# Low halves of the context keys in the recurrence stage: made by GpSimd in place of VectorE

## The chip, the cores and the metric

The kernel runs on one core of a Trainium2 chip. The metric is the device time of one execution in microseconds (us). Five engines work side by side on the core: TensorE (PE in the profile), VectorE (DVE), ScalarE (ACT), GpSimd (POOL) and SyncE (SP), which here issues the DMAs. Each runs its own instructions in order and waits on semaphores for what other engines made.

## The reference, cut to what matters

The program is four layers in a row. Layer 0 is a recurrent layer over 4 sequences of 512 positions; layers 1, 2 and 3 attend to a context of 1601 positions of width 512 for each sequence (layer 3 to the context and its own 512 latents together). The stage that is changed computes the recurrence of layer 0 and, beside it, the keys and values that the three attention layers need of the context.

```python
# layer 0: state s (head, 16, 16), one step per position
def step(s, rkvw):
    r_t, k_t, v_t, w_t = rkvw
    a = k_t[:, :, :, None] * v_t[:, :, None, :]
    out = jnp.einsum('bhk,bhkd->bhd', r_t, u * a + s)
    return (a + w_t[:, :, :, None] * s, out)
...
# layer 1: keys and values of the normalised context
a = _layer_norm(audio_kv, ln_gamma, ln_beta)
K = (a @ Wk.T); V = (a @ Wv.T)
# layer 2: of the context itself, eight key heads of 16
k = encoder_hidden_state @ Wk + bk
v = encoder_hidden_state @ Wv + bv
# layer 3: of the context itself
kv = h @ kv_w + kv_b
```

## The kernel before, in words

The program is a chain of stages, each a block of its own with a barrier behind it. The changed one is `scan_and_keys` (L1087). Two streams of work share its engines.

The first is the recurrence, in 256 steps (`STEPS`, 16 for each of 16 pieces of sequence and channel chunk; the pieces are numbered q). Step n handles 128 channels by 512 positions of one state column. TensorE spreads a value row over the partitions (`scan_vb`, L1282). VectorE multiplies it by the key (`outer`, `scan_a`, L1581, one operand in PSUM) and runs the scan over the 512 positions (`scan`, `scan_states`, L1588, operands in SBUF). GpSimd multiplies the state by the receptance (`weigh_state`, `scan_z`, L1511, operands in SBUF), and TensorE sums four of those products at a time (`reduce_four`, `scan_acc`, L1299). ScalarE seeds the first column of each state buffer two steps ahead (`seed`, L1376). There are `SR` = 4 state buffers, so the scan of step n waits for the product of step n-4, the seed of step n+2 for the product of step n-2, and the sum of products 4g to 4g+3 stands in TensorE's order at step 4g+5.

The second stream makes keys and values of the context. The 1601 positions of a sequence are cut into three tiles of 512 and one of 65, so there are 16 tiles, twelve full ones and four short. For each tile TensorE runs groups of float16 matmuls into one of three PSUM banks: `k2`, four `v2`, `std`, four `k3`, the `mean` of the next tile, four `v3`, four `k1`, four `v1` (`group_order`, L1057). The matmuls take float32 numbers as two float16 halves, a high one (the number rounded) and a low one (what is left). ScalarE drains each bank twice for a key: once in float32 (`scan_kf`, `scan_k2f`, L1384) and once rounded to float16 (`scan_hi`, `scan_k2hi`, L1385). `key_low` then subtracts the two and writes the low half in float16 (`scan_lo`, `scan_k2lo`, L1644). It is called once per key and tile: for k3 and k1 over 4 x n numbers a partition, for k2 over n. SyncE stores both halves (`keys_out`, L1203), and ScalarE may overwrite `kf` once the low half is made (semaphore `halves`).

Other work of the second stream on VectorE is the low half of the raw tile (`scan_xl`, L1625), centring (`scan_xc`, L1620), the reciprocal of the deviation (`scan_std`, L1630), the scaling by it (`scan_xc`, L1632) and the low half of the normalised tile (`a_low`, `scan_al`, L1637). On GpSimd it is the sum of channel chunks for mean and deviation: `add_pairs` (`scan_pairsum`, L1517) and `add_halves` (`scan_total`, L1524).

The order is written out by hand. `when[t, group, m]` gives every group a step by its share of TensorE's work, and each engine has a generator `keys` that yields the step at which its next piece is due. An engine first issues its part of the recurrence for step n and then whatever is due, so a piece stands behind the product or the scan of its step in the engine's order. The yields of one generator come in a fixed sequence: a piece whose step is earlier than the one before it in the generator still comes behind it. The places that matter are `yield when[t.t, "k3", C - 1] + 2`, `yield when[t.t, "k1", C - 1] + 2` and `yield when[t.t, "k2", 0] + 2`.

Of the kernel before, what the change touches and what calls it, by code (L numbers as in the profile page):

```python
# [7 lines left out]
ALU, ACT, AX = mybir.AluOpType, mybir.ActivationFunctionType, mybir.AxisListType  # L8
# [3 lines left out]
C = E // P  # L12
# [1074 lines left out]
def scan_and_keys(nc, w, k):  # L1087


    with ExitStack() as ctx:  # L1090
# [4 lines left out]
        tiles = [Stretch(t) for t in range(B * TILES)]  # L1095
        LAST = len(tiles) - 1

        ends, when, cost, count = {}, {}, {}, 0
# [12 lines left out]
        def end(t, what, m=None):  # L1111
            return ends[t, what, {"k": C - 1, "v": len(tiles[t].width) - 1}[what[0]] if m is None and what != "k2" else m or 0]
# [19 lines left out]
        xc, kf = ph.sb("xc", [P, C, KT]), ph.sb("kf", [P, C, KT])  # L1132
        hi, lo = ([ph.sb(f"{n}{i}", [P, C, KT], F16) for i in range(2)] for n in ("hi", "lo"))
        k2f, k2hi, k2lo = ph.sb("k2f", [P, 1, KT]), ph.sb("k2hi", [P, 1, KT], F16), ph.sb("k2lo", [P, 1, KT], F16)
# [19 lines left out]
        product, drained, copied = ph.sem("product"), ph.sem("drained"), ph.sem("copied")  # L1154
        staged, whigh, wlow = [ph.sem(f"staged{i}") for i in range(6)], ph.sem("whigh"), ph.sem("wlow")
        arrived = [ph.sem(f"arrived{i}") for i in range(2)]
        centred, squared, inverted, normed, scaled = (ph.sem(n) for n in ("centred", "squared", "inverted", "normed", "scaled"))
        paired, totalled = ph.sem("paired"), ph.sem("totalled")
        xhigh, xsplit, asplit, halves = ph.sem("xhigh"), ph.sem("xsplit"), ph.sem("asplit"), ph.sem("halves")
        kstored = {n: ph.sem(f"stored_{n}") for n in ("k1", "k2", "k3")}  # L1160
# [13 lines left out]
        with nc.Block() as block:  # L1174
# [329 lines left out]
            @block.gpsimd  # L1504
            def _(pool):
                def weigh_state(n):
                    pool.wait_ge(scanned, n + 1)
                    pool.wait_ge(seeded, n + 1)
                    if n >= ZR:
                        pool.wait_ge(reduced, (n - ZR) // 4 + 1)  # L1510
                    nc.gpsimd.tensor_tensor(Z[n % ZR][:], src["r"][n // HS % 2][:], S[n % SR][:, 0:T], ALU.mult).then_inc(zdone, 1)  # L1511

                def add_pairs(t, nth):
                    n, done = t.n, 2 * t.t + nth
                    if done:
                        pool.wait_ge(totalled, done)
                    nc.gpsimd.tensor_tensor(pairsum[:, :, 0:n], x[t.t % 2][:, 0:2, 0:n], x[t.t % 2][:, 2:4, 0:n], ALU.add).then_inc(paired, 1)  # L1517

                def add_halves(t, nth):
                    n, done = t.n, 2 * t.t + nth  # L1520
                    pool.wait_ge(paired, done + 1)
                    if t.t:
                        pool.wait_ge(product, end(t.t - 1, ("mean", "std")[nth], 0))
                    nc.gpsimd.tensor_tensor(total[nth][:, 0:n], pairsum[:, 0, 0:n], pairsum[:, 1, 0:n], ALU.add).then_inc(totalled, 1)  # L1524

                def keys():
                    yield 6
                    pool.wait_ge(arrived[0], 16)
                    add_pairs(tiles[0], 0)
                    add_halves(tiles[0], 0)  # L1530
                    yield 11
                    pool.wait_ge(squared, 1)
                    add_pairs(tiles[0], 1)
                    add_halves(tiles[0], 1)
                    for t in tiles[1:]:
                        before = tiles[t.t - 1]
                        yield when[before.t, "k3", 0]
                        pool.wait_ge(arrived[t.t % 2], 16 * (t.t // 2 + 1))
                        add_pairs(t, 0)
                        yield when[before.t, "k3", 0] + 1  # L1540
                        add_halves(t, 0)
                        yield when[before.t, "k1", 2] + 3
                        pool.wait_ge(squared, t.t + 1)
                        add_pairs(t, 1)
                        yield when[before.t, "k1", 2] + 4
                        add_halves(t, 1)

                more = keys()
                due = next(more)
                for n in range(STEPS + AFTER):  # L1550
                    if n < STEPS:
                        weigh_state(n)
                    while due is not None and due <= n:
                        due = next(more, None)

            @block.vector
            def _(dve):
# [50 lines left out]
                def weight_low(j):  # L1608
                    name, stage = stages[j]
                    dve.wait_ge(whigh, j + 1)  # L1610
                    nc.vector.scalar_tensor_tensor(W[name].lo[:], stage, WSCALE, W[name].hi[:], ALU.mult, ALU.subtract).then_inc(wlow, 1)
# [24 lines left out]
                    dve.wait_ge(scaled, 2 * C * (t.t + 1))  # L1636
                    nc.vector.tensor_tensor(as_.lo[:, :, 0:n], xc[:, :, 0:n], as_.hi[:, :, 0:n], ALU.subtract).then_inc(asplit, 1)  # L1637

                def key_low(t, name, full, hi_, lo_):
                    n = t.n  # L1640
                    dve.wait_ge(drained, end(t.t, name))
                    if t.t:
                        dve.wait_ge(kstored[name], 32 * t.t)
                    nc.vector.tensor_tensor(lo_[:, :, 0:n], full[:, :, 0:n], hi_[:, :, 0:n], ALU.subtract).then_inc(halves, 1)  # L1644

                def keys():
                    for j in range(4):
                        yield STAGE_AT[j]
                        weight_low(j)
                    yield 9  # L1650
                    centre(tiles[0])
                    yield 10
                    x_low(tiles[0])
                    yield STAGE_AT[4]
                    weight_low(4)
                    yield STAGE_AT[5]
                    weight_low(5)
                    for t in tiles:
                        yield when[t.t, "k2", 0] + 2
                        key_low(t, "k2", k2f, k2hi, k2lo)  # L1660
                        yield when[t.t, "std", 0] + 2
                        normalise(t)
                        yield when[t.t, "k3", C - 1] + 2
                        key_low(t, "k3", kf, hi[0], lo[0])
                        yield when[t.t, "v3", min(1, len(t.width) - 1)] + 2
                        a_low(t)
                        if t.t < LAST:
                            yield when[t.t, "k1", 0]
                            x_low(tiles[t.t + 1])
                            yield when[t.t, "k1", 0] + 1  # L1670
                            centre(tiles[t.t + 1])
                        yield when[t.t, "k1", C - 1] + 2
                        key_low(t, "k1", kf, hi[1], lo[1])

                outer(0)
                more = keys()
                due = next(more)
                for n in range(STEPS + AFTER):
# [2457 lines left out]
```

## Time and profile before

| what | value |
|---|---|
| time, median of 3 runs | 5353.01 us (5352.04 to 5363.05) |
| the profiled execution | 5354.71 us |
| its span, first to last instruction | 5352.7 us |
| first scan of the stage starts, last one starts | 431.1 us, 1341.5 us |
| busy over the whole span: PE, DVE, ACT, POOL | 4758.5, 3731.0, 2930.4, 2071.8 us |
| granted TensorE clock, mean over the span | 0.946 |

The stage takes about 915 us of the 5352.7. A busy time is the time in which the engine had an instruction begun and not ended. For VectorE and GpSimd an instruction can be begun and stand still, so its recorded length is more than its work; the rows below show this. The idle time before an instruction is put down to the engine that released it.

### The profile page before, as it was taken

To read this page: it belongs to the slowest core of one execution; us is meant where nothing else is said; L and a number is where in the kernel's file an instruction comes from. 1 tells how busy PE (TensorE), PEld (TensorE's weight loads), DVE (VectorE), ACT (ScalarE), POOL (GpSimd) and SP (SyncE) were. 2 spreads that over 40 slices of the span, in tenths; PEclk is the share of its full clock that TensorE was granted. 3 is DMA by queue.
4 is the path that set the end of the run, shared out by engine and by line. 5 is a ranking of instruction groups with operands and counts; after the bars stand their busy time and mean duration, and the time that the engine had idled before them with its cause. 6 is when DMAs were issued, how large, how long until landed. Compare 5 with 4: busy or idle time off the path is not lost. (4 is left out here: it accounts for less than half of the span.)

```text
span 5352.7 us, 75036 instructions
## 1 busy us (share of the span) xinstructions
PE 4758.5 (89%) x28626; PEld 1687.4 (32%) x28626; DVE 3731.0 (70%) x4661; ACT 2930.4 (55%) x5439; POOL 2071.8 (39%) x924
## 2 busy tenths in 40 slices
PE   5995988999378799997899999997899999996899
PEld 2342433334133233332322222222343333331344
DVE  5658999999565677771599999993457777771431
ACT  2443444444344366664288888885226666665442
POOL 0005666666131388775000000000007888886000
PEclk9997999999699799998999999998999999998999
DMA  2334344343301433323211111112424233221200
GB/s 98 132 117 128 114 109 112 104 114 98 114 32 48 89 69 69 71 58 104 75 29 33 34 34 32 34 30 70 112 75 102 60 68 71 60 49 68 71 24 16
DMA packets 474607, 391.60 MB, mean 73 GB/s; under 512 B 174895, under 2 KB 372372, under 8 KB 474216
## 3 DMA queue, kind: packets, MB, share of 16 engines
q1 hardware_dynamic: 474240, 386.74, 26.7%
q8 instruction: 227, 3.72, 0.3%
q14 instruction: 140, 1.15, 0.1%
HBM read 246.24 MB, written 139.34 MB: 72 GB/s over the span
## 5 line engine op out<-in xcount | busy, mean ns | idle before, releaser
L2941 DVE TENSOR_REDUCE att_part<-att_scores 128x2 f32<-128x802 f32 x1024 | 953.6, 987 | 112.0 <-PE att_scores L2780 100.2
L2914 ACT ACTIVATE att_prob<-att_lower 128x512 f32<-128x512 f32 (+1 forms) x1664 | 883.7, 596 | 132.2 <-PE att_lower L2794 110.9
L3711 DVE TENSOR_REDUCE att_part<-att_scores 128x1 f32<-128x423 f32 x1280 | 676.0, 590 | 240.9 <-PE att_scores L3442 240.7
L3655 ACT ACTIVATE att_prob<-att_lower 128x512 f32<-128x512 f32 (+1 forms) x1088 | 563.2, 602 | 243.9 <-PE att_lower L3454 242.1
L3695 POOL TENSOR_TENSOR att_acc<-att_acc,att_prob 128x1024 f32<-128x1024 f32 (+2 forms) x240 | 671.3, 2797 | 51.6 <-ACT att_prob L3655 22.4
L2517 DVE TENSOR_REDUCE att_part<-att_scores 128x1 f32<-128x401 f32 x1024 | 515.3, 567 | 162.0 <-PE att_scores L2331 161.9
L1511 POOL TENSOR_TENSOR scan_z<-scan_r,scan_states 128x512 f32<-128x512 f32 x256 | 469.7, 1839 | 360.0 <-DVE scan_states L1588 347.9
L2809 PE MATMUL att_lower<-att_prob,att_v 128*32 128x256 f32 (+1 forms) x6144 | 526.0, 415 | 19.7 <-issue 19.7
L2456 ACT ACTIVATE att_prob<-att_scores 128x512 f32<-128x512 f32 (+1 forms) x832 | 430.7, 601 | 195.3 <-PE att_scores L2343 195.3
L2928 POOL TENSOR_TENSOR att_out<-att_sums_sb,att_spread 128x512 f32<-128x512 f32 x32 | 40.7, 1272 | 1170.5 <-DMA att_spread<-recips 1170.5
L2497 POOL TENSOR_TENSOR att_acc<-att_acc,att_prob 128x1024 f32<-128x1024 f32 (+2 forms) x176 | 450.3, 2559 | 68.6 <-ACT att_prob L2456 56.2
L2780 PE MATMUL att_scores<-att_k,att_q 48*128 48x401 f16 x2048 | 426.0, 341 | 29.1 <-DVE att_part L2941 25.5
L3442 PE MATMUL att_scores<-att_k,att_q 97*128 97x423 f16 x1280 | 434.9, 347 | 12.0 <-DVE att_part L3711 11.6
L2794 PE MATMUL att_lower<-att_q,att_k 49*128 49x512 f16 (+1 forms) x1664 | 421.5, 389 | 8.6 <-ACT att_prob L2914 1.5
L1588 DVE TENSOR_TENSOR_SCAN scan_states<-scan_w,scan_initial,scan_a 128x512 f32<-128x512 f32 x256 | 425.1, 1661 | 0.0
L3454 PE MATMUL att_lower<-att_q,att_k 98*128 98x512 f16 (+1 forms) x1088 | 409.6, 383 | 13.5 <-ACT att_prob L3655 7.6
L2331 PE MATMUL att_scores<-att_k,att_q 97*128 97x401 f16 x1024 | 357.6, 353 | 28.6 <-DMA att_q<-in_c_q 28.3
L2343 PE MATMUL att_scores<-att_q,att_k 98*128 98x512 f16 (+1 forms) x832 | 312.0, 382 | 6.3 <-ACT att_prob L2456 6.1
L3465 PE MATMUL att_lower<-att_prob,att_v 128*32 128x512 f32 (+1 forms) x2176 | 289.6, 604 | 0.0
L2354 PE MATMUL att_sums<-att_prob,att_v 128*32 128x512 f32 (+1 forms) x1664 | 221.4, 604 | 0.0
L3695 POOL TENSOR_TENSOR att_acc<-att_prob 128x2048 f32<-128x2048 f32 x16 | 72.6, 4537 | 374.4 <-ACT att_prob L3655 374.4
L3442 PEld LDWEIGHTS att_scores<-att_k,att_q 97*128 97x128 f16 x1280 | 124.7, 97 | 279.6 <-DVE att_part L3711 174.2
(397 smaller groups left out, 7875.8 us busy)
## 6 DMA issues: line engine op xcount, KB each, us to landing
v<-scan_val SPq DMA_DIRECT2D x96, 256.0 KB, 2.3
att_v<-v SPq DMA_DIRECT2D x32, 768.0 KB
att_spread<-recips SPq DMA_DIRECT2D x64, 256.0 KB
mix_plane<-in_mask SPq DMA_DIRECT2D x16, 800.5 KB, 6.5
att_k<-k1hi SPq DMA_DIRECT2D x32, 400.2 KB
att_k<-k3hi SPq DMA_DIRECT2D x32, 400.2 KB
scan_x<-in_ctx_t SPq DMA_DIRECT2D x12, 1024.0 KB, 6.0
o<-att_out SPq DMA_DIRECT2D x32, 256.0 KB, 2.0
```

The source lines that it names most:

```text
L1511: nc.gpsimd.tensor_tensor(Z[n % ZR][:], src["r"][n // HS % 2][:], S[n % SR][:, 0:T], ALU.mult).then_inc(zdone, 1)
L2456: nc.scalar.activation(prob[g % NP][0:kw(kt), h, :], scores2[0:kw(kt), n % RING2, :], ACT.Exp).then_inc(exped, 1)
L2497: nc.gpsimd.tensor_tensor(acc[s % 2][0:kw(kt), heads], so_far[0:kw(kt), heads], prob[g % NP][0:kw(kt), heads], ALU.add).then_inc(padded, 1)
L2517: nc.vector.reduce_max(part[q % 2][:, hc, piece:piece + 1], scores1[:, bank["piece", p], 0:PIECE], AX.X).then_inc(reduced, 1)
L2780: ins = nc.tensor.matmul(scores1[:, b, a, 0:PIECE], Q[i][r, e, c * P:(c + 1) * P], K[i][r, k0:k0 + PIECE], start=True, stop=True)
L2809: ins = nc.tensor.matmul(sums[32 * h:32 * h + 32, cols], V[s % 2][0:kw(kt), kt, :], prob[g % NP][0:kw(kt), h, cols], start=kt == 0, stop=k ...
L2914: nc.scalar.activation(prob[g % NP][0:kw(kt), h, :], scores2[0:kw(kt), n % RING2, :], ACT.Exp).then_inc(exped, 1)
L2941: nc.vector.reduce_max(part[q % 2][:, :, ec, piece], scores1[:, bank["unit", p], :, 0:PIECE], AX.X).then_inc(reduced, 1)
L3442: nc.tensor.matmul(scores1[:, b, 0:PIECE], Q[i][0:TOP, h, c * P:(c + 1) * P], K[i][0:TOP, h, k0:k0 + PIECE], start=True, stop=True).then_i ...
L3655: nc.scalar.activation(prob[g % NP][0:kw(kt), h, :], scores2[0:kw(kt), n % RING2, :], ACT.Exp).then_inc(exped, 1)
L3695: nc.gpsimd.tensor_tensor(acc[s % 2][0:kw(kt), heads], so_far[0:kw(kt), heads], prob[g % NP][0:kw(kt), heads], ALU.add).then_inc(padded, 1)
L3711: nc.vector.reduce_max(part[q % 2][:, hc, piece:piece + 1], scores1[:, bank["piece", p], 0:PIECE], AX.X).then_inc(reduced, 1)
```

## The change

`key_low` moves from VectorE's block to GpSimd's, with the same operands and the same semaphores, and so do its three calls for each tile. GpSimd's generator now runs over all tiles with the key halves at the steps that they had on VectorE. VectorE's generator loses them.

```diff
--- before.py
+++ after.py
@@ -1516,6 +1516,13 @@
                         pool.wait_ge(totalled, done)
                     nc.gpsimd.tensor_tensor(pairsum[:, :, 0:n], x[t.t % 2][:, 0:2, 0:n], x[t.t % 2][:, 2:4, 0:n], ALU.add).then_inc(paired, 1)
 
+                def key_low(t, name, full, hi_, lo_):
+                    n = t.n
+                    pool.wait_ge(drained, end(t.t, name))
+                    if t.t:
+                        pool.wait_ge(kstored[name], 32 * t.t)
+                    nc.gpsimd.tensor_tensor(lo_[:, :, 0:n], full[:, :, 0:n], hi_[:, :, 0:n], ALU.subtract).then_inc(halves, 1)
+
                 def add_halves(t, nth):
                     n, done = t.n, 2 * t.t + nth
                     pool.wait_ge(paired, done + 1)
@@ -1532,18 +1539,26 @@
                     pool.wait_ge(squared, 1)
                     add_pairs(tiles[0], 1)
                     add_halves(tiles[0], 1)
-                    for t in tiles[1:]:
-                        before = tiles[t.t - 1]
-                        yield when[before.t, "k3", 0]
-                        pool.wait_ge(arrived[t.t % 2], 16 * (t.t // 2 + 1))
-                        add_pairs(t, 0)
-                        yield when[before.t, "k3", 0] + 1
-                        add_halves(t, 0)
-                        yield when[before.t, "k1", 2] + 3
-                        pool.wait_ge(squared, t.t + 1)
-                        add_pairs(t, 1)
-                        yield when[before.t, "k1", 2] + 4
-                        add_halves(t, 1)
+                    for before in tiles:
+                        t = tiles[before.t + 1] if before.t < LAST else None
+                        yield when[before.t, "k2", 0] + 2
+                        key_low(before, "k2", k2f, k2hi, k2lo)
+                        if t:
+                            yield when[before.t, "k3", 0]
+                            pool.wait_ge(arrived[t.t % 2], 16 * (t.t // 2 + 1))
+                            add_pairs(t, 0)
+                            yield when[before.t, "k3", 0] + 1
+                            add_halves(t, 0)
+                        yield when[before.t, "k3", C - 1] + 2
+                        key_low(before, "k3", kf, hi[0], lo[0])
+                        if t:
+                            yield when[before.t, "k1", 2] + 3
+                            pool.wait_ge(squared, t.t + 1)
+                            add_pairs(t, 1)
+                            yield when[before.t, "k1", 2] + 4
+                            add_halves(t, 1)
+                        yield when[before.t, "k1", C - 1] + 2
+                        key_low(before, "k1", kf, hi[1], lo[1])
 
                 more = keys()
                 due = next(more)
@@ -1636,13 +1651,6 @@
                     dve.wait_ge(scaled, 2 * C * (t.t + 1))
                     nc.vector.tensor_tensor(as_.lo[:, :, 0:n], xc[:, :, 0:n], as_.hi[:, :, 0:n], ALU.subtract).then_inc(asplit, 1)
 
-                def key_low(t, name, full, hi_, lo_):
-                    n = t.n
-                    dve.wait_ge(drained, end(t.t, name))
-                    if t.t:
-                        dve.wait_ge(kstored[name], 32 * t.t)
-                    nc.vector.tensor_tensor(lo_[:, :, 0:n], full[:, :, 0:n], hi_[:, :, 0:n], ALU.subtract).then_inc(halves, 1)
-
                 def keys():
                     for j in range(4):
                         yield STAGE_AT[j]
@@ -1656,12 +1664,8 @@
                     yield STAGE_AT[5]
                     weight_low(5)
                     for t in tiles:
-                        yield when[t.t, "k2", 0] + 2
-                        key_low(t, "k2", k2f, k2hi, k2lo)
                         yield when[t.t, "std", 0] + 2
                         normalise(t)
-                        yield when[t.t, "k3", C - 1] + 2
-                        key_low(t, "k3", kf, hi[0], lo[0])
                         yield when[t.t, "v3", min(1, len(t.width) - 1)] + 2
                         a_low(t)
                         if t.t < LAST:
@@ -1669,8 +1673,6 @@
                             x_low(tiles[t.t + 1])
                             yield when[t.t, "k1", 0] + 1
                             centre(tiles[t.t + 1])
-                        yield when[t.t, "k1", C - 1] + 2
-                        key_low(t, "k1", kf, hi[1], lo[1])
 
                 outer(0)
                 more = keys()
```

Nothing else is touched: TensorE, ScalarE and SyncE keep their instructions and their order. What stands in a row on GpSimd is shown for the second full tile of the stage, from the `k2` half to the next one (`scan_z` is the product of a step, a count behind a row says how often it stands there in succession). Before:

```order
L1511 TENSOR_TENSOR scan_z<-scan_r,scan_states 128x512 x12
L1517 TENSOR_TENSOR scan_pairsum<-scan_x 128x1024
L1511 TENSOR_TENSOR scan_z<-scan_r,scan_states 128x512
L1524 TENSOR_TENSOR scan_total<-scan_pairsum 128x512
L1511 TENSOR_TENSOR scan_z<-scan_r,scan_states 128x512 x4
L1517 TENSOR_TENSOR scan_pairsum<-scan_x 128x2x65
```

And in the changed kernel:

```order
L1511 TENSOR_TENSOR scan_z<-scan_r,scan_states 128x512 x4
L1524 TENSOR_TENSOR scan_lo<-scan_kf,scan_hi 128x2048
L1511 TENSOR_TENSOR scan_z<-scan_r,scan_states 128x512 x8
L1517 TENSOR_TENSOR scan_pairsum<-scan_x 128x1024
L1511 TENSOR_TENSOR scan_z<-scan_r,scan_states 128x512
L1531 TENSOR_TENSOR scan_total<-scan_pairsum 128x512
L1524 TENSOR_TENSOR scan_lo<-scan_kf,scan_hi 128x2048
L1511 TENSOR_TENSOR scan_z<-scan_r,scan_states 128x512 x4
L1524 TENSOR_TENSOR scan_k2lo<-scan_k2f,scan_k2hi 128x512
```

The twelve products in a row are cut after the fourth by the `k3` half. The `k1` half stands behind the sums of the next tile's squares and one product more than on VectorE, and the `k2` half ahead of the next `scan_pairsum`. On VectorE, around the `k3` half of the second full tile (`scan_o` finishes a piece of the recurrence, `scan_bv` is its bonus term, `scan_al` the low half of the normalised tile), there stood:

```order
L1606 TENSOR_TENSOR scan_o<-scan_bv,scan_acc 128x512
L1644 TENSOR_TENSOR scan_lo<-scan_kf,scan_hi 128x2048
L1581 TENSOR_TENSOR scan_a<-scan_k,scan_vb 128x512
L1588 SCALAR_TENSOR_TENSOR scan_states<-scan_w,scan_initial,scan_a 128x512
L1600 TENSOR_TENSOR scan_bv<-scan_v,scan_vb 128x512
L1581 TENSOR_TENSOR scan_a<-scan_k,scan_vb 128x512
L1588 SCALAR_TENSOR_TENSOR scan_states<-scan_w,scan_initial,scan_a 128x512
L1637 TENSOR_TENSOR scan_al<-scan_xc,scan_ah 128x2048
```

And in the changed kernel, where the lines of VectorE's block have moved down by 15:

```order
L1621 TENSOR_TENSOR scan_o<-scan_bv,scan_acc 128x512
L1596 TENSOR_TENSOR scan_a<-scan_k,scan_vb 128x512
L1603 SCALAR_TENSOR_TENSOR scan_states<-scan_w,scan_initial,scan_a 128x512
L1615 TENSOR_TENSOR scan_bv<-scan_v,scan_vb 128x512
L1596 TENSOR_TENSOR scan_a<-scan_k,scan_vb 128x512
L1603 SCALAR_TENSOR_TENSOR scan_states<-scan_w,scan_initial,scan_a 128x512
L1652 TENSOR_TENSOR scan_al<-scan_xc,scan_ah 128x2048
```

The low half of the keys is gone, and what stood behind it follows in the same order. (The program's listing names the scan a SCALAR_TENSOR_TENSOR; the profile calls it TENSOR_TENSOR_SCAN.)

## Rows read from the trace of the kernel before

**Rows 1.** Windows: two full tiles of the third sequence, and fourteen tiles summed:
```profile
core 0: us, PE busy (x) PEld busy (x) DVE busy (x) ACT busy (x) POOL busy (x), PEclk, DMA share, GB/s
978.88:1041.00 62.12, 59.74 (x320) 25.03 (x319) 61.12 (x49) 28.42 (x58) 43.62 (x22) 1.00 0.38 107
1041.00:1103.02 62.02, 58.62 (x303) 24.71 (x302) 54.74 (x48) 25.12 (x61) 36.61 (x25) 0.92 0.40 116
...
sum 781.40, PE 719.30 PEld 304.10 DVE 728.05 ACT 341.21 POOL 520.02; mean PE 51.38 PEld 21.72 DVE 52.00 ACT 24.37 POOL 37.14
```

**Rows 2.** Waits of DVE and PE, 500 to 1340 us: us, times, longest:
```profile
DVE scan_a L1581 <- PE scan_vb L1282: 31.8, 21, 5.2
...
PE scan_psum L1310 <- DVE scan_al L1637: 29.9, 15, 4.5
PE scan_acc L1299 <- POOL scan_z L1511: 20.3, 11, 3.7
PE scan_psum L1310 <- POOL scan_total L1524: 11.2, 3, 4.0
```

**Rows 3.** Groups by form, DVE: busy us, mean ns of one:
```profile
L1644 DVE TENSOR_TENSOR scan_lo<-scan_kf,scan_hi 128x2048 f16<-128x2048 f32 x24 | 56.8, 2368 | 0.0
...
L1644 DVE TENSOR_TENSOR scan_k2lo<-scan_k2f,scan_k2hi 128x512 f16<-128x512 f32 x12 | 15.4, 1283 | 1.0 <-ACT scan_k2hi L1385 1.0
```

**Rows 4.** Timeline of DVE: start us, length us (idle before, releaser):
```profile
812.97 1.73 DVE L1588 TENSOR_TENSOR_SCAN scan_states<-scan_w,scan_initial,scan_a 128x512 f32<-128x512 f32 x1
814.62 2.26 DVE L1644 TENSOR_TENSOR scan_lo<-scan_kf,scan_hi 128x2048 f16<-128x2048 f32 x1
...
817.40 1.70 DVE L1588 TENSOR_TENSOR_SCAN scan_states<-scan_w,scan_initial,scan_a 128x512 f32<-128x512 f32 x1
...
819.80 2.52 DVE L1588 TENSOR_TENSOR_SCAN scan_states<-scan_w,scan_initial,scan_a 128x512 f32<-128x512 f32 x1
...
823.03 1.43 DVE L1588 TENSOR_TENSOR_SCAN scan_states<-scan_w,scan_initial,scan_a 128x512 f32<-128x512 f32 x1
...
825.17 1.44 DVE L1588 TENSOR_TENSOR_SCAN scan_states<-scan_w,scan_initial,scan_a 128x512 f32<-128x512 f32 x1
...
869.46 1.72 DVE L1588 TENSOR_TENSOR_SCAN scan_states<-scan_w,scan_initial,scan_a 128x512 f32<-128x512 f32 x1
...
871.89 1.72 DVE L1588 TENSOR_TENSOR_SCAN scan_states<-scan_w,scan_initial,scan_a 128x512 f32<-128x512 f32 x1
```

**Rows 5.** Timeline of POOL, the same stretch:
```profile
812.34 1.28 POOL L1511 TENSOR_TENSOR scan_z<-scan_r,scan_states 128x512 f32<-128x512 f32 x1 [1.16 <-DVE scan_states L1588]
814.78 3.23 POOL L1511 TENSOR_TENSOR scan_z<-scan_r,scan_states 128x512 f32<-128x512 f32 x1 [1.16 <-DVE scan_states L1588]
817.97 3.27 POOL L1517 TENSOR_TENSOR scan_pairsum<-scan_x 128x1024 f32<-128x1024 f32 x1
```

**Rows 6.** Timeline of POOL in a later stage, VectorE not beside it:
```profile
1442.35 4.06 POOL L893 TENSOR_TENSOR ffn_asl<-ffn_att,ffn_ash 128x2048 f16<-128x2048 f32 x1 [2.02 <-ACT ffn_ash L760]
...
1496.21 4.51 POOL L884 TENSOR_TENSOR ffn_att<-ffn_att,ffn_g 128x2048 f32<-128x2048 f32 x1 [17.14 <-ACT ffn_g L88]
```

**Rows 7.** Groups by form, POOL, in an attention stage:
```profile
L2497 POOL TENSOR_TENSOR att_acc<-att_acc,att_prob 128x1024 f32<-128x1024 f32 x128 | 302.3, 2361 | 40.5 <-ACT att_prob L2456 28.7 <-POOL att_acc L2497 0.4
```

**Rows 8.** Timeline of PE behind a k1 half:
```profile
1045.68 1.93 PE L1299 MATMUL scan_acc<-scan_z,scan_red 128*32 128x512 f32 x8 [3.18 <-POOL scan_z L1511]
```

**Rows 9.** Timeline of DVE, the same place:
```profile
1051.62 0.69 DVE L1581 TENSOR_TENSOR scan_a<-scan_k,scan_vb 128x512 f32<-128x512 f32 x1 [3.29 <-PE scan_vb L1282]
...
1056.02 3.35 DVE L1630 RECIPROCAL scan_std<-scan_std 128x512 f32<-128x512 f32 x1
```

**Rows 10.** Timeline of POOL, the same place:
```profile
1056.01 1.27 POOL L1511 TENSOR_TENSOR scan_z<-scan_r,scan_states 128x512 f32<-128x512 f32 x1
```

**Rows 11.** Windows of 5 us across that wait (columns of rows 1):
```profile
1041.00:1046.00 5.00, 1.82 (x21) 1.16 (x23) 4.79 (x6) 1.02 (x4) 5.00 (x4) 0.87 0.62 205
1046.00:1051.00 5.00, 5.00 (x38) 2.67 (x30) 1.99 (x2) 1.67 (x5) 5.00 (x4) 0.50 0.39 89
```

## The prediction

> **What bounds the kernel now.** I read the windows by tile first, then the waits, then the timelines of VectorE and GpSimd side by side.
>
> In the windows the reader is to see that two engines look full at once [rows 1]. In the first full tile shown TensorE is busy 59.74 of 62.12 us and VectorE 61.12; in the second, which prepares the short tile, 58.62 and 54.74 of 62.02; over fourteen tiles 719.3 and 728.05 of 781.4. GpSimd with 520 looks to have 261 us to spare. The waits say that the bound changes hands [rows 2]: VectorE waits 31.8 us for spread values, TensorE 29.9 for the low half of the normalised tile, 20.3 for products of GpSimd and 11.2 for its totals.
>
> Whether GpSimd's idle time can be had is told by the timelines, with starts and lengths added up. A product of GpSimd takes 1.28 us where nothing is beside it and 3.23 us where VectorE's key half of 2.26 us starts 0.16 us before it [rows 4, 5]. The scan behind it is begun at 817.40, but the product ends at 818.01 and the scan at 819.10: it has run for 1.09. Next GpSimd's `scan_pairsum` ends at 821.24 and the scan begun at 819.80 ends at 822.32, 1.08 later. So two operations that each read two operands of SBUF, one on each engine, take turns, and the recorded length of the one holds the other's work. `outer`, with an operand in PSUM, and the reciprocal run beside GpSimd freely: a product that starts with the reciprocal takes its 1.27 [rows 9, 10].
>
> This shared turn is what I budget. A scan and a product together hold it 2.15 us: the scans at 823.03 and 825.17 end at 824.46 and 826.61, where GpSimd is behind and always has the next product ready [rows 4]. Where it is not behind, a step takes 2.43 (ends at 871.18 and 873.61), as 0.28 goes between a scan's end and its product. The key half on VectorE makes the step 4.40 (814.70 to 819.10), so it holds the turn 2.25 and costs the step 1.97, since it hides the 0.28.
>
> **The change part by part.** Removed from VectorE: 24 full halves, 56.8 us recorded, 12 of k2, 15.4 us [rows 3], and eight and four of the short tiles. By the steps above the full ones cost 24 x 1.97 = 47 us of VectorE's time.
>
> Added to GpSimd: the same. The operation with these types and shape is in the trace: 4.06 us [rows 6]. GpSimd's 1024-column sum takes 2.36 alone [rows 7] and holds the turn 2.14 (819.10 to 821.24) [rows 4, 5], so 0.22 of it is outside; I take 4.06 - 0.22 = 3.84 for the key half. That is 1.6 us more of the turn than on VectorE. For k2 no row has the form; a quarter of 4.06 less the same 0.22 is 0.8, and a product of that size holds the turn 1.07 (2.15 less the scan's 1.08), against a quarter of 2.25: 0.2 to 0.5 us more.
>
> The Trainium skill, GPSIMD Engine Reference, section 3.1 (Elementwise, side by side), gives 4497 ns for a float32 tensor_tensor of 2048 against 2293 on VectorE. The trace has 4.51 for the float32 form too, but 4.06 for the form with the float16 output [rows 6]. By 4.5 us a full half would cost 0.44 us more, 11 us over 24.
>
> The k3 half, replayed from the end of the scan ahead of it, with GpSimd level. Before: scan ends at 4.40, at 6.83, and, with `scan_al` of the same length between, at 11.2. After: 2.43; then the half holds the turn until 6.27; scan 7.35, the product that was held up 8.4, `scan_al` 10.7, product 11.7, scan 12.8. That is 1.6 later with GpSimd in the same state, so nothing absorbs it: three more two-operand pieces follow at once. Eight of the twelve full tiles are full of turns like the first one shown. The four ahead of a short tile have it open for some microseconds (54.74 of 62.02) and their sums are small, so I count half: 8 x 1.6 + 4 x 0.8 = 16 us.
>
> The k1 half with the k2 half behind it. Before, on VectorE: product 3.3, scan 4.4, `scan_pairsum` 6.5, scan 7.6, product 8.7, scan 9.8, total 10.8, scan 11.9, next product 13.0. After: scan 2.43, `scan_pairsum` until 4.6, scan 5.7, product 6.7, scan 7.8, total 8.9, scan 10.0, half until 13.8, scan 14.9, next product 16.0, and then in turn, with GpSimd three products behind and the next scan held by the ring of four state buffers. VectorE comes to the reciprocal's step at about the time that it did before (+0.4 us), as the turns without a half are 2.15 instead of 2.43 and longer. During the 3.35 us of the reciprocal [rows 9], which before was mostly idle turn, GpSimd works off what it owes, the k2 half with it. About one product of 1.07 is still owed, and I count half. So 0.95 for each full tile: 12 x 0.95 = 11 us.
>
> TensorE waits more. By that replay the first product behind the k1 half comes 3 us later than before (16.0 against 13.0). Queued behind the waiting sum are TensorE's groups and the next spreads, and for those waits VectorE. The place is in the trace: TensorE stands 3.18 us for that product [rows 8], its granted clock goes to 0.50 (1.2 of 2.4 GHz) [rows 11], and VectorE then stands 3.29 us for the spread [rows 9]. The sums come every fourth step and mostly have some slack; in three or four tiles they have less than the 3 us. ScalarE's seeds wait for the same products. What the ring already counts must not be counted twice: I take 4 us, with bounds 0 (all of it inside what the ring holds back) and 12 tiles x (3 + 1.5 for the clock) = 54.
>
> SyncE's stores wait for `halves` up to 6 us longer; they have half a tile until ScalarE asks for the buffer. I count nothing. If that cover went, ScalarE's drains would stand for it, which is in the bound of 54. The short tiles' halves have an eighth of the width: nothing.
>
> Sum: 16 + 11 + 4 = 31 us. The profiled execution took 5354.7 us around its span of 5352.7, so 5386; the median of before is 1.7 lower, so 5384 against 5353.0, 0.6% slower.
>
> **The rivals.** *Faster.* VectorE's queue sets the stage and GpSimd's extra turn is found in idle time: the reciprocals (12 x 3.35 = 40 us), VectorE's 31.8 us for spreads, the 0.28 of plain steps. For it: VectorE's 47 us really go, and `scan_al` stands behind them, for which TensorE waits 29.9 us [rows 2]. It decides where a half costs the step less than 1.97 on GpSimd. TensorE's own waits cap it, about 61 us [rows 2], and the longer waits for products eat half: 5353 - 30 = 5323. Against it: the k3 half has no idle turn behind it. 14%.
>
> *No difference.* TensorE bounds all tiles as it does the four (58.62 of 62.02), and 1 to 2 us more of turn a tile go into its shadow. Time: 5353, give or take 8. Against it: in the eight tiles VectorE has nearly no idle time. 15%.
>
> *Slower by twice as much.* The late products starve TensorE in every full tile, its clock falls to 0.50 each time, and each fall brings VectorE's wait as at 1051.62: 27 + 12 x 3 = 63, so 5353 - 2 + 63 = 5414. For it: this chain is in the trace already at the smaller backlog. Against it: only one of the sums in a tile stands at that place. 17%.
>
> *The engines don't take turns when GpSimd writes float16*, and the half runs beside the scan: then GpSimd is only late by 4 us, and the time is that of the first rival. It is in the 14%.
>
> **How the numbers follow.** The forecast has 54%, with 5366 to 5402 as its own range (k3 at half or one and a half of its term, TensorE's 0 to 12). A measurement of this kernel can tell about 0.2%, 11 us, from no change. Slower by more than that: 54 + 17, plus 1 from the edge of the third case, 72%. Within it 14%, faster 14%. The range of 8 in 10 leaves out the best part of the faster case and the tail of the worse one: 5345 to 5420.
>
> **What would show it.** Right: the sum of lengths of `scan_states` grows though their work is the same, as scans stand behind 4 us halves; the full halves on GpSimd show means of 4.9 to 5.2 us (3.84 plus a scan of 1.08 ahead); steps behind a k3 half take 4.9, not 2.43; VectorE's share falls by less than 47 us; TensorE's wait for `scan_z` grows from 20.3 to 30 us or more. Full tiles of the first kind become 2 to 3 us longer, and stages before and behind stay. Wrong: halves of 4.1 us with scans of 1.7 beside them, or tiles shorter than 62 us, or waits for `scan_al` that shrink by more than the products' grow.

## The result, and the profile after

The changed kernel takes 5418.9 us (median of 4 runs, 5412.3 to 5421.2) against 5352.5 for the kernel before: ratio 1.0115, 95% interval 1.0099 to 1.0131. It is 66 us slower, 53 to 70 by that interval. The prediction said 31 us slower, 5384, with 5345 to 5420 as its range. The direction and the shared turn were right, and the size was half of the measured one. 5419 lies 1 us inside the upper end of the range and far outside the forecast's own 5366 to 5402.

All of it is in the recurrence stage. From the first scan's end to the last one's the stage takes 976.6 us against 910.4 in the profiled executions; what lies before and behind it agrees within 1 us. The windows over the same two full tiles, the short one behind them and the fourteen tiles of [rows 1], for the changed kernel (cut here from scan end to scan end, there from start to start, which shifts a tile's length by up to 2 us):

```profile
core 0: us, PE busy (x) PEld busy (x) DVE busy (x) ACT busy (x) POOL busy (x), PEclk, DMA share, GB/s
...
1011.58:1080.10 68.52, 64.28 (x327) 26.68 (x326) 59.73 (x44) 29.74 (x61) 50.56 (x26) 0.95 0.38 108
1080.10:1151.15 71.05, 62.95 (x345) 26.69 (x343) 58.71 (x45) 25.65 (x63) 45.52 (x28) 0.93 0.36 105
1151.15:1184.92 33.77, 20.29 (x151) 8.79 (x151) 21.71 (x21) 12.21 (x38) 16.37 (x11) 0.75 0.30 85
...
sum 849.46, PE 739.31 PEld 311.87 DVE 713.78 ACT 340.47 POOL 604.62; mean PE 52.81 PEld 22.28 DVE 50.98 ACT 24.32 POOL 43.19
```

The tiles went from 62.12 and 62.02 to 68.52 and 71.05 us, the short one from 30.21 to 33.77, and the fourteen from 781.4 to 849.5. VectorE is busy 14 us less over these fourteen tiles and 19 less over the whole stage, not 47. The loss is uneven, both kernels taken from scan end to scan end: next to nothing in the first tile of a sequence, 5 to 6 us in the second, 8 to 11 in the third, which stands ahead of the short one, and 3 to 3.5 in three of the four short ones.

VectorE's scans grew though their work is the same, from 425.1 us over 256 to 465.7 (groups by form, VectorE, then GpSimd; `x256` counts the instructions, then come busy us and mean ns of one):

```profile
L1603 DVE TENSOR_TENSOR_SCAN scan_states<-scan_w,scan_initial,scan_a 128x512 f32<-128x512 f32 x256 | 465.7, 1819 | 0.7 <-POOL scan_z L1511 0.7
```
```profile
L1524 POOL TENSOR_TENSOR scan_lo<-scan_kf,scan_hi 128x2048 f16<-128x2048 f32 x24 | 115.3, 4803 | 0.0
...
L1524 POOL TENSOR_TENSOR scan_k2lo<-scan_k2f,scan_k2hi 128x512 f16<-128x512 f32 x12 | 18.4, 1536 | 0.0
```

Of the full halves on GpSimd 19 last 4.97 to 5.08 us, with a scan ahead of them, and five 4.06 or 4.07, without one.

TensorE's waits (us in total, times, longest):

```profile
PE scan_psum L1310 <- DVE scan_al L1652: 31.3, 16, 4.6
PE scan_acc L1299 <- POOL scan_z L1511: 28.9, 11, 6.1
PE scan_psum L1310 <- ACT scan_k2hi L1385: 25.1, 9, 5.0
PE scan_psum L1310 <- POOL scan_total L1531: 24.5, 3, 8.4
```

The first, the second and the fourth answer to [rows 2]. The third was, before:

```profile
PE scan_psum L1310 <- ACT scan_k2hi L1385: 6.2, 4, 3.3
```

The wait for products grew from 20.3 to 28.9, but the totals' from 11.2 to 24.5 and the wait for ScalarE's drain of `k2hi` from 6.2 to 25.1. Step by step in the trace, TensorE stands behind 11 of the 12 full k1 halves: six times for `k2hi` (3.1 to 5.0 us), twice for a product (6.0 and 6.1), and three times, in the short tiles, for a total (8.0 to 8.4). Before, it stood 0.8 to 4.0 us at seven of these places. VectorE's own wait for spread values went from 31.8 to 101.5 us.

**The k3 half, as a turn.** The timelines of VectorE and of GpSimd around one (start, length, idle before it in brackets):

```profile
1110.95 1.72 DVE L1603 TENSOR_TENSOR_SCAN scan_states<-scan_w,scan_initial,scan_a 128x512 f32<-128x512 f32 x1
1113.81 0.69 DVE L1596 TENSOR_TENSOR scan_a<-scan_k,scan_vb 128x512 f32<-128x512 f32 x1 [1.14 <-PE scan_vb L1282]
1114.42 3.21 DVE L1603 TENSOR_TENSOR_SCAN scan_states<-scan_w,scan_initial,scan_a 128x512 f32<-128x512 f32 x1
```
```profile
1111.55 4.99 POOL L1524 TENSOR_TENSOR scan_lo<-scan_kf,scan_hi 128x2048 f16<-128x2048 f32 x1
```

The half is issued at 1111.55 and stands behind the scan that ends at 1112.67. It ends at 1116.54, 3.87 us later (forecast 3.84). The next scan was begun at 1114.42 and ends at 1117.63, 1.09 after the half. From scan to scan that is 4.96 us (forecast 4.92).

**The k1 half, and what stands behind it.** GpSimd, TensorE, ScalarE and VectorE at the same step of the stage as in [rows 8 to 10]:

```profile
1081.12 4.98 POOL L1524 TENSOR_TENSOR scan_lo<-scan_kf,scan_hi 128x2048 f16<-128x2048 f32 x1
1086.07 5.86 POOL L1511 TENSOR_TENSOR scan_z<-scan_r,scan_states 128x512 f32<-128x512 f32 x4
```
```profile
1088.30 1.93 PE L1299 MATMUL scan_acc<-scan_z,scan_red 128*32 128x512 f32 x8 [6.02 <-POOL scan_z L1511]
```
```profile
1088.27 0.20 ACT L1376 ACTIVATE scan_states<-scan_initial 128x1 f32<-128x1 f32 x1 [8.54 <-POOL scan_z L1511]
```
```profile
1093.69 0.69 DVE L1596 TENSOR_TENSOR scan_a<-scan_k,scan_vb 128x512 f32<-128x512 f32 x1 [6.50 <-PE scan_vb L1282]
```

TensorE stands 6.02 us where it stood 3.18, and VectorE 6.50 where it stood 3.29. ScalarE stands 8.54 us on a seed and drains no bank meanwhile. The windows across it give the granted clock (columns as above):

```profile
1084.00:1088.00 4.00, 0.00 (x0) 0.00 (x0) 3.19 (x1) 0.00 (x0) 4.00 (x2) 0.74 0.24 80
1088.00:1094.00 6.00, 5.71 (x46) 3.22 (x47) 0.31 (x1) 2.26 (x8) 5.46 (x6) 0.60 0.55 143
```

TensorE does nothing for 4 us and then works at 0.60 of its clock for 6, a mean of its two levels of 1.2 and 2.4 GHz. The time at the lower level, from the first scan's end to the last one's, went from 104 to 163 us.

ScalarE has one new wait besides. It stands 8.9 us in total, in three places, until GpSimd has made a low half and `kf` may be overwritten; before it never stood for that.

### The profile page after: what moved, and what is told of

It reads as the page before. It is cut to its first block and busy times, and to the rows that moved or that the text cites. A ratio compares the mean times of both kernels' runs of the same rounds, so it can differ in the third digit from the quotient of the medians.

```text
span 5418.8 us, 75036 instructions
## 1 busy us (share of the span) xinstructions
PE 4773.8 (88%) x28626; PEld 1694.7 (31%) x28626; DVE 3711.5 (68%) x4613; ACT 2929.3 (54%) x5439; POOL 2169.9 (40%) x972
## 5 line engine op out<-in xcount | busy, mean ns | idle before, releaser
L1511 POOL TENSOR_TENSOR scan_z<-scan_r,scan_states 128x512 f32<-128x512 f32 x256 | 434.9, 1706 | 327.0 <-DVE scan_states L1603 324.7
L1603 DVE TENSOR_TENSOR_SCAN scan_states<-scan_w,scan_initial,scan_a 128x512 f32<-128x512 f32 x256 | 465.7, 1819 | 0.7 <-POOL scan_z L1511 0.7
L1596 DVE TENSOR_TENSOR scan_a<-scan_k,scan_vb 128x512 f32<-128x512 f32 x256 | 174.7, 683 | 116.2 <-PE scan_vb L1282 103.9
```

The costliest lines, as they stand in the source:

```text
L1603: nc.vector.tensor_tensor_scan(S[n % SR][:, 1:], src["w"][q % 2][:], A[n % 2][:], s0[:, q, lane(i):lane(i) + 1], ALU.mult, ALU.add).then_i ...
```

## The experiments

All were timed in five rounds against the kernel before on the same chip. Ratios are to it, with 95% intervals. The length of the stage, first scan's end to last one's, is from one profiled execution of each. Where halves are made on two engines, each kind of key has a semaphore of its own in place of the shared count.

**Each kind of half alone.** First k3: VectorE has k2 and k1 again, GpSimd keeps k3. VectorE's generator:

```diff
+                        yield when[t.t, "k2", 0] + 2
+                        key_low(t, "k2", k2f, k2hi, k2lo)
...
+                        yield when[t.t, "k1", C - 1] + 2
+                        key_low(t, "k1", kf, hi[1], lo[1])
```

> The k3 low halves on GpSimd, k1 and k2 low halves on VectorE as before; each kind of key has a semaphore of its own, as two engines now count. Theory A (a half on GpSimd costs its longer hold of the turn that both engines share, 3.84 against 2.25 us): 12 x about 1.3 us = 15 us, 5368 us. Theory B (the cost is that products stand behind the half on GpSimd, so TensorE and ScalarE run dry and the clock falls; in the changed kernel the steps behind a k3 half show none of it): the same 15 us here, 5368. Rival C (VectorE's relief counts): below 5350.

Measured: 5365.8 us, 1.0033 (1.0021 to 1.0046), 16 us slower (11 to 25 by the interval); the stage is 15.0 us longer. The run does not separate A from B, and C falls. The three steps behind a k3 half are together 1.5 to 1.8 us longer than before in eight of the twelve full tiles, 0.7 in three, and 0.2 shorter in the first. That makes 14.7 us.

Then the k1 halves alone, with the same kind of edit:

> The k1 low halves on GpSimd, k3 and k2 on VectorE. Theory A: 12 x 1.6 us = 19 us, 5372. Theory B: the k1 half stands between the sums of squares and the products that TensorE's sums and ScalarE's seeds wait for, so most of the 50 us that are left of the 66: 35 to 50 us, 5388 to 5402, with TensorE's waits for k2hi and for totals as in the changed kernel. Rival C: below 5350.

Measured: 5386.4 us, 1.0074 (1.0060 to 1.0087), 36 us slower; the stage is 38.9 us longer. Its waits of TensorE:

```profile
PE scan_psum L1312 <- ACT scan_k2hi L1387: 26.8, 9, 6.2
...
PE scan_psum L1312 <- POOL scan_total L1533: 16.7, 3, 6.1
```

The wait for `k2hi` is there in full with the k1 half alone, the one for totals only in part (24.5 in the change). B is right on the time, A would have had half.

And the k2 halves alone:

> The k2 low halves on GpSimd, k3 and k1 on VectorE. Theory A: 12 x 0.2 to 0.5 us, 2 to 6 us, 5355 to 5359. Theory B: the k2 half stands ahead of the sum of the next tile, which TensorE's mean group needs, but it is short: 0 to 10 us. If the k2 half is what delays the totals in the changed kernel, 15 us or more.

Measured: 5363.3 us, 1.0026 (1.0014 to 1.0037), 13 us slower, which is more than either theory gave and nearest to the last case, late totals; the stage is 12.5 us longer. TensorE waits 19.6 us for totals there, 11.2 before. The three add up: 16 + 36 + 13 = 65 of the 66 us, each known to 6 or 7 us. In the traces the stage grew by 15.0 + 38.9 + 12.5 = 66.4 of 66.2 us. So I explain them one by one.

**The k2 half behind the sum.** In the change it stands ahead of the next tile's `scan_pairsum` and `scan_total`, here behind them:

```diff
-                        yield when[before.t, "k2", 0] + 2
-                        key_low(before, "k2", k2f, k2hi, k2lo)
                         if t:
                             yield when[before.t, "k3", 0]
...
                             add_pairs(t, 0)
                             yield when[before.t, "k3", 0] + 1
                             add_halves(t, 0)
+                        yield when[before.t, "k2", 0] + 2
+                        key_low(before, "k2", k2f, k2hi, k2lo)
```

> The k2 half alone on GpSimd, as in the run of k2 only, but behind the sum of the next tile instead of ahead of it. The hold is the same. If the 13 us of k2 only are what stood behind it (TensorE's wait for totals 19.6 us there, 11.2 before): 5350 to 5358, with that wait back at about 11. If they are the hold or k2's own lateness: 5360 to 5366.

Measured: 5352.9 us, 1.0002 (0.9993 to 1.0011), no difference from before, and the wait for totals:

```profile
PE scan_psum L1312 <- POOL scan_total L1533: 11.4, 3, 4.0
```

The stage is 0.4 us longer than before. So the k2 half itself costs nothing that the interval shows, and its 13 us were its place ahead of a sum that TensorE waits for. It is the place, not the time that the half takes. In the run with k2 ahead, 10.7 of the stage's 12.5 us are lost in three of the short tiles, where the half has 65 columns. GpSimd in one of them, from product 125 of the stage on, with k2 ahead of the sum and then behind it:

```profile
885.03 1.28 POOL L1513 TENSOR_TENSOR scan_z<-scan_r,scan_states 128x512 f32<-128x512 f32 x1 [1.16 <-DVE scan_states L1601]
887.47 1.28 POOL L1513 TENSOR_TENSOR scan_z<-scan_r,scan_states 128x512 f32<-128x512 f32 x1 [1.16 <-DVE scan_states L1601]
890.04 1.26 POOL L1513 TENSOR_TENSOR scan_z<-scan_r,scan_states 128x512 f32<-128x512 f32 x1 [1.29 <-DVE scan_states L1601]
891.26 0.50 POOL L1526 TENSOR_TENSOR scan_k2lo<-scan_k2f,scan_k2hi 128x65 f16<-128x65 f32 x1
891.72 2.33 POOL L1519 TENSOR_TENSOR scan_pairsum<-scan_x 128x1024 f32<-128x1024 f32 x1
894.13 2.06 POOL L1533 TENSOR_TENSOR scan_total<-scan_pairsum 128x512 f32<-128x512 f32 x1
```
```profile
882.11 1.28 POOL L1513 TENSOR_TENSOR scan_z<-scan_r,scan_states 128x512 f32<-128x512 f32 x1 [1.16 <-DVE scan_states L1601]
883.35 3.26 POOL L1519 TENSOR_TENSOR scan_pairsum<-scan_x 128x1024 f32<-128x1024 f32 x1
886.58 2.17 POOL L1513 TENSOR_TENSOR scan_z<-scan_r,scan_states 128x512 f32<-128x512 f32 x1
888.72 1.45 POOL L1533 TENSOR_TENSOR scan_total<-scan_pairsum 128x512 f32<-128x512 f32 x1
```

The half takes 0.50 us. But in a short tile it is due two steps after the next tile's sum, and as the yields of one generator come in a fixed sequence, the sum waits for the half's step: `scan_pairsum` stands behind product 127 and not 125, and the total ends 11.16 us after product 125 begins and not 8.06. TensorE's longest wait for totals went from 4.0 to 7.1 us. The changed kernel has the sum behind product 127 too.

**Length of the hold, k3.** Half the width, the order unchanged. The kernel leaves out half of the k3 low numbers of the full tiles:

```diff
-                    nc.gpsimd.tensor_tensor(lo_[:, :, 0:n], full[:, :, 0:n], hi_[:, :, 0:n], ALU.subtract).then_inc(halves, 1)
+                    c = C // 2 if n == KT else C
+                    nc.gpsimd.tensor_tensor(lo_[:, 0:c, 0:n], full[:, 0:c, 0:n], hi_[:, 0:c, 0:n], ALU.subtract).then_inc(halves[name], 1)
```

> The k3 half alone on GpSimd and only two of its four channel chunks in full tiles; the other two chunks are left out (zeros are stored for them). The run of k3 only was 16 us slower than before. If that is the hold of the shared turn, a hold of about 1.8 us in place of 3.84 takes 12 x 2.0 = 24 us off: 5340 to 5348, a little faster than before. If it is GpSimd's order or start-up and not the length: 5358 to 5366.

Measured: 5343.2 us, 0.9988 (0.9979 to 0.9997), 23 us less than with the whole half. The recorded length went from 4999 to 3051 ns, 1.95 us; times 12 that is 23.4 us, and the stage is 23.7 us shorter. The three steps behind the half became 1.9 us shorter in all but one tile, and the others moved little. For the k3 half the price is the length of the hold.

**Length of the hold, k1.** The same edit with the k1 half alone on GpSimd.

> The k1 half alone on GpSimd and only two of its four channel chunks in full tiles; the other two are left out (zeros are stored). The run of k1 only was 36 us slower than before. Hold alone: 24 us less, 5362 to 5368. Queue theory: the products behind it come 2 us earlier too and fit into the slack that TensorE's sums have, so more than 24 us less: 5340 to 5358.

Measured: 5356.7 us, 1.0013 (1.0004 to 1.0022), 30 us less than with the whole half, where the hold accounts for 23. The times alone, with their intervals, hardly tell 30 from 23; the stage is 34.8 us shorter in the traces, and the wait for `k2hi` fell from 26.8 to 11.7. So a microsecond of the k1 half costs more than one: what is queued behind it counts too.

**The k1 half at the reciprocal.** Its float32 copy gets a buffer `kg` of its own, and its store moves with it:

```diff
-xc, kf = ph.sb("xc", [P, C, KT]), ph.sb("kf", [P, C, KT])
+xc, kf, kg = ph.sb("xc", [P, C, KT]), ph.sb("kf", [P, C, KT]), ph.sb("kg", [P, C, KT])
...
                             add_halves(t, 0)
+                        if before.t:
+                            yield when[before.t, "std", 0] + 2
+                            key_low(tiles[before.t - 1], "k1", kg, hi[1], lo[1])
```

> The k1 half alone on GpSimd, as in the run of k1 only, but with a float32 buffer of its own, placed six products later, behind the sum of the next tile, where VectorE is at its reciprocal (3.35 us without the turn). The hold is the same 3.84 us. Theory A: as k1 only where the hold must be found, 5375 to 5390. Theory B (late products and totals at the old place): most of the 36 us go, and the hold falls on an idle turn: 5335 to 5360.

Measured: 5367.7 us, 1.0025 (1.0016 to 1.0035), 14 us slower than before. 22 of the 36 us went, but not as many as B said, 5335 to 5360. The edit moves the half and gives it a buffer, so ScalarE's wait of 8.4 us until `kf` is free is gone too; what each is worth alone was not run. One half there, GpSimd first, then VectorE:

```profile
1056.33 4.07 POOL L1529 TENSOR_TENSOR scan_lo<-scan_kg,scan_hi 128x2048 f16<-128x2048 f32 x1
```
```profile
1054.94 3.32 DVE L1649 RECIPROCAL scan_std<-scan_std 128x512 f32<-128x512 f32 x1
1058.30 4.25 DVE L1651 TENSOR_TENSOR scan_xc<-scan_xc,scan_std 128x2048 f32<-128x2048 f32 x1
```

It begins 1.4 us into the reciprocal and ends 2.1 us behind it, and the scaling (2.3 us alone) stands for those. In four tiles the half falls on the reciprocal of a short tile, 0.55 us. TensorE's wait for `scan_al` is 48.0 us there, against 29.9: a half that no longer delays products delays the normalised tile. That this wait is what the 14 us are is read from the trace and was not tested.

**Six state buffers**, on the changed kernel and on the one before:

```diff
-        SR, ZR, VR, CR, PB = 4, 8, 4, 3, 5
+        SR, ZR, VR, CR, PB = 6, 8, 4, 3, 5
```

> The changed kernel with six state buffers in place of four, so that ScalarE's seed of step n+2 waits for the product of step n-4 instead of n-2 and may run past a half on GpSimd. Theory A (the longer hold of the shared turn alone): no change against the changed kernel, 5410 to 5420. Theory B1 (late products cost through ScalarE: seeds, then drains, then TensorE's banks): TensorE's 25 us of waits for k2hi go, 20 to 40 us back, 5375 to 5400. Theory B2 (late products cost through TensorE's own sums and the totals): little comes back, 5405 to 5420, and the wait for scan_z stays near 33 us.

Measured: 5398.8 us, 1.0087 (1.0073 to 1.0101), 20 us better than the change. ScalarE's wait for products fell from 182.5 to 5.5 us and TensorE's for `k2hi` from 25.1 to none, so B1 is right, at the low end of its 20 to 40 us. The stage is 19.4 us shorter. Less came back than the 25 us of waits that went, and the waits for products (37.6) and totals (28.5) have grown.

> The kernel before with six state buffers, the control of the run with six buffers on the changed kernel. TensorE waited only 6 us for k2hi here, so by all theories 0 to 10 us faster, 5342 to 5352.

Measured: 5349.3 us, 0.9995 (0.9986 to 1.0004), no difference.

**All halves on GpSimd, out of the way**: the three edits above together, k3 as it was.

> All halves on GpSimd as in the change, but nothing waits behind them if it can be helped: six state buffers, k1 with a float32 buffer of its own and placed behind the sum of the next tile, k2 behind that sum too, k3 where it is. Hold theory alone (all of the 66 us): 5405 to 5420. Queue theory: the 16 us of k3 stay, k1 leaves the 14 us of its run at the reciprocal, k2 0 to 5: 5380 to 5390. If halves close together disturb each other: 5390 to 5405.

Measured: 5388.9 us, 1.0072 (1.0058 to 1.0086), 39 us slower than before and 27 us faster than the change, with the same instructions of the halves. It is what k3 (16), k1 at the reciprocal (14) and k2 behind the sums (3, no difference by its interval) add up to, and 6 more, whose cause stays open; TensorE waits 51.5 us for `scan_al` there. Hold alone is refuted.

**The halves in pieces.**

```diff
+                        for c in range(C):
+                            yield when[before.t, "k1", C - 1] + 2 + (c if before.n == KT else 0)
+                            key_piece(before, "k1", kf, hi[1], lo[1], c)
```

> All halves on GpSimd as in the changed kernel, but k1 and k3 halves of full tiles in four pieces of 512 columns, one piece a step, so that at most one piece stands ahead of a product. The hold is the same in sum or a little longer (four instructions for one). Theory A: as the changed kernel or up to 10 us more, 5415 to 5430. Theory B: the late products go, what is left is the longer hold, 16 + 19 us: 5380 to 5395.

Measured: 5429.9 us, 1.0149 (1.0135 to 1.0163), as A said, but the trace shows another cause, a new wait that the edit brought:

```profile
ACT scan_xh L1409 <- POOL scan_lo L1531: 71.0, 12, 8.0
```

ScalarE waits for the whole k3 half ahead of the next tile's high half, and the last piece now comes three steps later. The run tells nothing about late products.

**The opposite move**, sums to VectorE, halves back on it:

```diff
-                    nc.gpsimd.tensor_tensor(pairsum[:, :, 0:n], x[t.t % 2][:, 0:2, 0:n], x[t.t % 2][:, 2:4, 0:n], ALU.add).then_inc(paired, 1)
+                    nc.vector.tensor_tensor(pairsum[:, :, 0:n], x[t.t % 2][:, 0:2, 0:n], x[t.t % 2][:, 2:4, 0:n], ALU.add).then_inc(paired, 1)
```

> The opposite move: key halves on VectorE as before, and the sums of channel chunks (scan_pairsum, scan_total) moved from GpSimd to VectorE at their steps. Shared turn (A, and B with it): a sum of 1024 holds the turn 2.14 us on GpSimd and about 1.1 on VectorE, one of 512 1.07 and 0.6, so 12 x 2 x 1.5 = 37 us less hold, products and totals come earlier, and VectorE's longer queue costs nothing while the turn is the bound: 10 to 35 us faster, 5315 to 5340. Rival (VectorE's queue is the bound, as its 95% busy suggests): 12 x 2 x 1.7 = 41 us more work on it, 5370 to 5395.

Measured: 5376.9 us, 1.0047 (1.0033 to 1.0061), 24 us slower. My theory of the turn as the only budget failed here, and the time lies in the range of the rival, VectorE's queue. The wait for products halved to 10.5 us, but this one grew from 11.2:

```profile
PE scan_psum L1310 <- DVE scan_total L1617: 37.6, 9, 8.0
```

The sum stands behind reciprocal and scaling in VectorE's order, and in the first tile of each sequence these come later, as the deviation stands two groups of k3 later on TensorE. Those four tiles are 5 to 8 us longer and the rest of the stage is even in sum. A full queue as such would show in all full tiles. How much of the 37 us of hold was really saved, and lost again as GpSimd no longer runs behind (steps of 2.43 in place of 2.15), was not separated.

## Why the prediction was half right

**The shared turn** is right, in size too. The k3 half's hold was forecast as 3.84 us and is 3.87, the step behind it as 4.92 and is 4.96, and the half-width run takes off 1.95 us for each half and 12 times that for the stage. This is also why the faster rival failed: of VectorE's 47 us of relief 19 are left in its busy time over the stage, as the scans wait.

**The k3 term** said 16 us. The run with k3 alone measured 16. That it agrees so closely is partly luck: 1.6 us in eight tiles and half of that in the four ahead of a short one were 1.2 and 1.3 on average.

**The k1 term and TensorE's term are the steps that failed.** "So 0.95 for each full tile: 12 x 0.95 = 11 us" and "I take 4 us, with bounds 0 [...] and [...] 54" were 15 us together for k1 and k2. They measured 36 and 13. The replay counted turns and closed the account at the reciprocal, with one product owed. It left out that others stand in line for those products while they are owed. Moving the k2 half behind the sums takes its 13 us to within the noise of nothing at the same hold, the k1 half at another place and with a buffer of its own gives back 22, six state buffers 20. I had named the chain and its bound (54) and then taken the low end, on the count of "three or four tiles" in which TensorE's sums have less than 3 us of slack; TensorE stood 3 to 8 us behind eleven halves. Of its added waits only 9 us are for products. 19 are for `k2hi`, which ScalarE could not drain while it stood on a seed; I had this in one sentence without a price, and the six buffers show it. 13 are for totals, delayed by the k1 half (16.7 us of such waits with it alone) and by the k2 half's step (19.6, against 11.2 before); I had no term for them.

**"The short tiles' halves have an eighth of the width: nothing"** looked at the width and not at the order. Three of the four short tiles lost 3 to 3.5 us each, and the run with k2 alone loses 2.9 to 4.0 in the same three, by the sum that came two products later. The full tiles ahead of a short one lost the most, 8 to 11 us. TensorE had the least room in them before (58.62 of 62.02 us busy, VectorE 54.74), and it is TensorE that late products and totals stop; this last step is argued.

**The signs.** Two of those named for being right did not come: the second tiles of a sequence grew by 5 to 6 us and the first ones by nothing, not 2 to 3, and the wait for products reached 28.9 and not 30. The halves' mean is 4.80, just under 4.9. They pointed at what was missing, the waits other than for products.

**The buffer** `kf` was counted as nothing, and ScalarE waits 8.9 us for it, 8.4 with the k1 half alone. What of this reaches the time was not separated.

**The clock** was put at 1.5 us a fall. Time at the lower level grew by 59 us; at half speed that is about 29 us of TensorE's work, an estimate from the rows, part of which lies beside other waits. It was not isolated.

**The rival "slower by twice as much"** gave 5414 by this mechanism and is the closest of all (its sum, 27 + 36 on 5353, is 5416: 2 us were taken off twice). Its evidence, the chain already visible before the change, was in the rows and was worth more than 17%. That the measured time is inside the range of 5345 to 5420, by 1 us, is luck: no term of the forecast reached it, only the tail left for this rival.

No version here beats the kernel before. The half-width k3 run does by 0.1%, but leaves work out.

## What to carry to other kernels

Where VectorE and GpSimd both read two SBUF operands, budget their holds as one resource: an idle GpSimd is not spare capacity, and an operation that takes 4.06 us there for 2.26 on VectorE makes the sum longer. Then price a moved instruction by what is queued behind it on its new engine and who waits for that: here a half of 0.50 us, 65 columns wide, cost 3 to 4 us in each of three tiles when its call stood ahead of a sum, and nothing measurable behind it. Where the order is written as a sequence of steps, check at which step everything behind an inserted piece now comes, in the short tiles too. If a trace already shows a small stall along the chain that a change will lengthen, expect it in every place where the chain occurs and not in the few that a slack count picks.

## What the runs showed that I had not expected

A product that GpSimd owes is cheaper in turn (2.15 us a step instead of 2.43) and much dearer through others: ScalarE lost 8.54 us at a single seed, one column wide. And taking from an engine that is busy 94% of the stage halves that cost it 47 us of steps moved its busy time by 19.
